# A graph attention layer on one core: where the constants of the attention scores are made

## What is computed

```python
self_feat = vcq @ W_self.T + b_self               # vcq: features and condition, 1024
for d in range(2):
    A = adj_f if d == 0 else swapaxes(adj_f, 1, 2)
    A = A[:, :, :20, :]                           # 20 keys
    qh = (self_feat @ Wq[d].T + bq[d]).reshape(B, N, 16, 32)
    kh = (self_feat[:, :20] @ Wk[d].T + bk[d]).reshape(B, 20, 16, 32)
    aff = einsum('bnhd,bmhd->bnhm', qh, kh) / sqrt(32)
    aff = where(A.sum(-1) > 0, aff, -9e15) + (A @ w_bias + b_bias)
    output += softmax(aff) applied to self_feat[:, :20] and Wout[d], + bout[d]
return x + relu(output)
```

## Time and profile before

| | us |
|---|---|
| median of 3 runs | 1914.61 (1913.51 to 1915.31) |
| profiled execution | 1915.0, span 1913.2, TensorE's mean granted clock 0.986 |
| TensorE matmuls busy | 1864.9 (97%) |
| TensorE weight loads busy | 1668.7 (87%) |
| VectorE, ScalarE, GpSimd busy | 1103.0, 1005.8, 725.4 |
| DMA | 255.59 MB, mean 134 GB/s |
| chain that ended last | TensorE 92% |
| of it L1562, L1575, L1542, L1540 | 30%, 20%, 10%, 3% |

### The profile page before, as it was taken

How to read it: one execution, slowest core, us unless ns; L and a number is a source line. 1 busy time by engine, 2 the same in 40 slices (tenths; PEclk the granted TensorE clock), 3 DMA queues, 4 the chain that set the end, 5 groups by cost and what they waited for, 6 DMA issues and landing times.

```text
span 1913.2 us, 46955 instructions
## 1 busy us (share of the span) xinstructions
PE 1864.9 (97%) x15864; PEld 1668.7 (87%) x15864; DVE 1103.0 (58%) x1937; ACT 1005.8 (53%) x1717; POOL 725.4 (38%) x617
## 2 busy tenths in 40 slices
PE   8999998879999999999999999999999999999997
PEld 5899998868888888888888888888888888888886
DVE  2433232456666666666666666666666666666632
ACT  2333232235556666666565566555666666656543
POOL 0322222004444444444444444444444444444444
PEclk9999999979999999999999999999999999999999
DMA  6123334444546565555555555565565555555431
GB/s 198 46 83 89 91 96 104 110 115 141 155 137 159 144 156 144 149 144 144 144 144 145 144 157 151 152 154 147 143 159 146 152 142 147 144 145 145 120 93 63
DMA packets 263747, 255.59 MB, mean 134 GB/s; under 512 B 78192, under 2 KB 194160, under 8 KB 263536
## 3 DMA queue, kind: packets, MB, share of 16 engines
q1 hardware_dynamic: 259360, 252.84, 49.4%
q10 hardware_dynamic: 4176, 0.02, 0.1%
HBM read 197.94 MB, written 54.79 MB: 132 GB/s over the span
## 4 chain that ended last, share of the span: by engine, by line
PE 92%; SPq 1%; DVE 1%; issue 1%; ACT 1%; DMA 0%; POOL 0%; POOLq 0%; DVEq 0%; ACTq 0%
PE bank L1562 30%; PE bank L1575 20%; PE low_banks L1542 10%; PE low_banks L828 9%; PE bank L1596 8%; PE bank L828 4%; PE bank L1588 4%; PE low_banks L1540 3%; PE bank L1563 2%; PE bank L1604 1%; SPq L640 1%; ACT kx L1437 0%; DVE zc L1267 0%; DMA k_dram<-kv_kst 0%; SPq L1078 0%
## 5 line engine op out<-in xcount | busy, mean ns | idle before, releaser
L1562 PE MATMUL bank<-kx,xt_main 128*128 128x160 f32 x4096 | 635.9, 304 | 0.3 <-ACT kx L1437 0.3
L1562 PEld LDWEIGHTS bank<-kx,xt_main 128*128 128x128 f32 x4096 | 583.8, 192 | 7.4 <-issue 0.9
L1437 ACT ACTIVATE kx<-low_banks 128x1280 f32<-128x1280 f32 (+3 forms) x268 | 318.2, 1187 | 259.1 <-PE low_banks L1542 259.1
L1388 POOL TENSOR_TENSOR res<-res,xk 128x512 f32<-128x512 f32 x128 | 163.9, 1280 | 669.6 <-ACT res L1427 669.6
L1280 DVE TENSOR_TENSOR sc<-bank,masks 128x320 f32<-128x320 f32 x256 | 125.8, 491 | 398.8 <-PE bank L1563 396.9
L1542 PE MATMUL low_banks<-key_tile,a_rows 32*128 32x160 f32 (+3 forms) x4288 | 220.7, 320 | 14.6 <-ACT kx L1437 8.9
L1575 PE MATMUL bank<-ws_h,xh_main 128*128 128x512 f32 x512 | 222.2, 434 | 2.5 <-DVE res L1306 2.5
L1370 POOL TENSOR_TENSOR sc<-sc,mx 128x640 f32<-128x640 f32 x128 | 160.2, 1272 | 152.1 <-DVE mx L1292 152.1
L1432 ACT ACTIVATE zc<-low_banks 128x1280 fp32r<-128x1280 f32 (+2 forms) x67 | 79.7, 1190 | 244.3 <-PE low_banks L1540 244.3
L1575 PE MATMUL bank<-ws_l,xh_main 128*128 128x512 f32 x512 | 203.1, 397 | 0.0
L1575 PE MATMUL bank<-ws_h,xl_main 128*128 128x512 f32 x512 | 203.0, 397 | 0.0
(11 more groups left out here) (144 smaller groups left out, 3085.4 us busy)
## 6 DMA issues: line engine op xcount, KB each, us to landing
rows_main<-in_x SPq DMA_DIRECT2D x256, 128.0 KB, 6.3
xs<-in_x SPq DMA_DIRECT2D x64, 512.0 KB, 4.8
xk<-in_x SPq DMA_DIRECT2D x64, 512.0 KB, 3.7
res<-c_dram SPq DMA_DIRECT2D x64, 512.0 KB, 7.2
out<-res SPq DMA_DIRECT2D x128, 256.0 KB, 3.1
adj<-in_mask_BxSxSx_ik SPq DMA_DIRECT2D x32, 440.0 KB, 8.2
adj<-in_mask_BxSxSx_ik SPq DMA_DIRECT2D x128, 110.0 KB
vbd<-v_dram SPq DMA_DIRECT2D x768, 10.0 KB
```

Source lines behind the costliest of these rows:

```text
L1388: pool.tensor_tensor(res[:, p.par, b, :], res[:, p.par, b, :], xk[:, p.par, b, :], ALU.add).then_inc(res_ready, 1)
L1437: nc.scalar.activation(taken(kx[:, t.par, j], lo, hi), generated(0, P, lo, hi), ACT.Copy).then_inc(gen_taken, 1)
L1562: mm = nc.tensor.matmul(dst, xt[:, j, p.ring + b, :], kx[:, t.par, j, :, :, w, :].rearrange("p r c m -> p c r m"), start=(j == 0), stop=False)
```

## The change

The constants are made in the keys stage. There the key is still in `kst`: ScalarE multiplies it by the query bias, GpSimd by the batch's condition query, both into `prod`. VectorE turns the blocks of 32 and sums 32 values each into `zs`; ScalarE and GpSimd split the sums into a high and a low part in `zz`; VectorE turns them so that they lie in rows, and SP stores them in `z_dram` with 8 DMAs at the end of each half, ahead of the next half's row loads. In the window loop step 0, its copy and its subtraction are gone, and so is `condition_columns`. Two DMAs a slot load four rows for each batch of the pair (`load_constants`) into `zc`, which now has four places and is cleared once. The order of the tiles in SBUF is another, and of the early loads those of the edges and of the first row sums come later: in half 7, behind the second key store (`late_loads`). The mask of the second edge direction is made by VectorE in slot -1.

```diff
@@ keys_and_values
+            sp.wait_ge(z_turned, n + 1)
+            for r in range(NQ):
+                for e in range(2):
+                    o = Q * r + ZQ * e
+                    sp.dma_start(v["z_dram"][r, e::2, bass.ds(n * HALF, HALF)].rearrange("c (q i) -> q c i", i=Q),
+                                 zt[o:o + MQ]).then_inc(z_stored, 16)
@@ SP, half 7
+                if last and p == 2:
+                    sp.wait_ge(pe_feat, C * HALVES)
+                    sp.wait_ge(f_low, C * HALVES)
+                    v["late_loads"](sp)
@@ VectorE
+        def constant_sums(n, p):
+            dve.wait_ge(by_bias, NK * n + p + 1)
+            dve.wait_ge(by_condition, NK * n + p + 1)
+            if due(NK * n + p):
+                dve.wait_ge(z_summed, NK * n + p)
+            nc.vector.transpose(pt[:], prod[:, p % 2].rearrange("p k (q i) -> p (k q) i", i=Q)).then_inc(p_turned, 1)
+            dve.wait_ge(p_turned, NK * n + p + 1)
...
+            nc.vector.tensor_reduce(zs[:, p].rearrange("p k q -> p (k q)"), pt[:], AX.X, ALU.add).then_inc(z_summed, 1)
+            constant_sums(n, 0)
+            for j in range(C):
+                constant_sums(n, 1 + j)
+                if not last:
                     features_out(n + 1, 1 - par, j)
+            constant_sums(n, 5)
             if not tail:
                 turn_x(blk + 1, n + 2, par)
...
                 nc.vector.transpose(vt[:, m % 4], vst[:, m % 2]).then_inc(v_turned, 1)
+                if m < 2:
+                    constant_sums(n, 6 + m)
+            turn_constants(n)
@@ GpSimd
+        def by_conditions(n, p):
+            pool.wait_ge(kv_out, 2 * NK * n + p + 1)
+            if due(NK * n + p - 1):
+                pool.wait_ge(p_turned, NK * n + p - 1)
+            pool.tensor_tensor(prod[:, p % 2, 1, :] ... kst ... cq ..., ALU.mult).then_inc(by_condition, 1)
+            by_conditions(n, 0)
+            by_conditions(n, 1)
             if not last:
                 conditions(n + 1)
-                features_low(n + 1, 1 - par)
+            for j in range(C):
+                by_conditions(n, 2 + j)
+                if not last:
+                    feature_low(n + 1, 1 - par, j)
+            by_conditions(n, 6)
+            by_conditions(n, 7)
...
+            constants_low(n)
@@ ScalarE
             if due(16 * (4 * n + p // 2)):
                 act.wait_ge(k_stored[p % 2], 16 * (4 * n + p // 2))
+            if due(NK * n + p - 1):
+                act.wait_ge(by_condition, NK * n + p - 1)
+                act.wait_ge(by_bias, NK * n + p - 1)
...
+        def by_biases(n, p):
+            act.wait_ge(kv_out, 2 * NK * n + p + 1)
+            if due(NK * n + p - 1):
+                act.wait_ge(p_turned, NK * n + p - 1)
+            nc.scalar.activation(prod[:, p % 2, 0, :], kst[:, p % 2, :], ACT.Copy,
+                                 scale=bq_all[:, p:p + 1]).then_inc(by_bias, 1)
             for j in range(C):
                 key_out(n, par, C + j)
+                by_biases(n, C + j)
                 if not last:
                     feature_high(n + 1, 1 - par, j)
@@ window_loop
+    def load_constants(sp, p):
+        for b in range(2):
+            o = (2 * p.n + b) * NG
+            sp.dma_start(zc[ZK * b:ZK * b + ZK, p.c % AGES, :].bitcast(F32).rearrange("k (h m) -> k h m", m=NG),
+                         v["z_dram"][:, :, bass.ds(o, NG)].rearrange("r (p k) m -> k (r p) m", k=ZK)
+                         ).then_inc(zc_loaded[p.par], 16)
@@ SP, slot
+                if t.back(4).real():
+                    sp.wait_ge(pe_s, scored(t.back(1), 3))
+                load_constants(sp, t)
@@ TensorE
-                pe.wait_ge(zl_ready, 2 * (t.n + 1) if t.real() else 2 * PAIRS)
-            elif step == 1:
-                pe.wait_ge(z_low, t.n + 1)
-                    if step == 0:
-                        mm = nc.tensor.matmul(low_banks[:, r, dst], zl[s, o, :], rhs, start=True, stop=True)
             if a == 0:
+                pe.wait_ge(zc_loaded[p.par], 32 * (p.half + 1))
-            if has_window(nxt):
-                generate(nxt, 0)
```

More of the change, by code:

```diff
@@ L141, in build @@
         kv_out = sem("kv_out")
+        z_stored = sem("z_stored")
         with ExitStack() as third:
-            windowed, early_loads, early_turn = window_loop(nc, scope(third)[0], sem, bank, low_banks, locals())
+            windowed, early_loads, late_loads, early_turn = window_loop(nc, scope(third)[0], sem, bank, low_banks, locals())
         with ExitStack() as keyed:
@@ L680, in turn_x, with turn_constants @@
                                 j).then_inc(x_turned, 1)
+        def constant_sums(n, p):
[5 more added lines that the diff above has]
+            dve.wait_ge(p_turned, NK * n + p + 1)
+            if p == 0 and due(n):
+                dve.wait_ge(z_high, n)
+                dve.wait_ge(z_low, n)
+            nc.vector.tensor_reduce(zs[:, p].rearrange("p k q -> p (k q)"), pt[:], AX.X, ALU.add).then_inc(z_summed, 1)
+        def turn_constants(n):
+            dve.wait_ge(z_low, n + 1)
+            if due(n):
+                dve.wait_ge(z_stored, 16 * 2 * NQ * n)
+            nc.vector.transpose(zt[:], zz[:].bitcast(F32).rearrange("p c h k q -> p (c h k q)")
+                                .rearrange("p (b i) -> p b i", i=Q)).then_inc(z_turned, 1)
         def one_half(blk, n, par, first, last, tail):
@@ L684, in one_half @@
                 pick_condition(n + 1)
-            if not last:
                 nonzero(n + 1, 1 - par)
-                for j in range(C):
+            constant_sums(n, 0)
+            for j in range(C):
+                constant_sums(n, 1 + j)
+                if not last:
                     features_out(n + 1, 1 - par, j)
+            constant_sums(n, 5)
             if not tail:
@@ L1135, in nonzero_rows @@
         spread = nzm[:].rearrange("p w z -> p (w z)")
-        for o in (0, Q):
-            a = p.ring * (P + 1) + o
-            nc.vector.tensor_scalar(spread[:, a:a + P + 2:P + 1], sums[:], 0.0, None,
+        for o in (1, 3):
+            a = p.ring * P + o
+            nc.vector.tensor_scalar(spread[:, a:a + P + ZK + 1:P + ZK], sums[:], 0.0, None,
                                     ALU.not_equal).then_inc(nz_ready, 1)
@@ L1260, in vector_program @@
     def vector_program(dve):
-        def constants_low(t):
-            dve.wait_ge(z_high, t.n + 1)
-            lo, hi = window(t)
-            o = taken(zc[Q:ZR, t.par], lo, hi)
-            nc.vector.tensor_tensor(o, generated(Q, ZR, lo, hi), o.bitcast(F32), ALU.subtract).then_inc(z_low, 1)
+        nc.vector.memset(zc[:].bitcast(F32), 0.0).then_inc(set_once, 1)
+        nc.vector.memset(nzm[:], 0.0).then_inc(set_once, 1)
+        dve.wait_ge(set_once, 2)
+        for b in range(2):
+            for o in (0, 2):
+                nc.vector.memset(nzm[:, b::2, ZK * b + o:ZK * b + o + 1], 1.0).then_inc(set_once, 1)
         def add_masks(t, a):
@@ L1309, in slot @@
             soft, late = t.back(3), t.back(4)
-            nxt, after = t.back(-1), t.back(-2)
+            nxt = t.back(-1)
             if soft.real():
@@ L1333, in slot @@
                 nonzero_rows(dve, nxt)
-            if after.real():
-                condition_columns(dve, after)
             g = edge_group(t if t.c % 2 == 0 else t.back(1))
-            if due(g) and has_edges(g):
+            if has_edges(g) and (due(g) or t.c % 2):
                 count_and_weigh(dve, g, t.c % 2)
```

158 lines of the change are left out of this document (86 added, 72 removed).

## The result

The kernel after takes 1925.47 us (median of 4 runs, 1923.86 to 1928.36), the kernel before 1914.06 (4 runs beside it): a ratio of 1.0063, 95% interval 1.0045 to 1.0080. It is slower, by 11.4 us; the interval is 8.6 to 15.3 us. The profiled execution of after took 1923.86 us with a span of 1922.0, against 1915.0 and 1913.2 of before.

The account below looks back on a forecast made before the run. The prediction took TensorE to bound both long stages. From the profiled 1915.0 us, -42.5 for the removed step and +61 for the keys stage, with zero for hand-over and loads, gave 1933.5 us, range 1897 to 1962.

Parts of the forecast that it names:

- a closed round on SP and the key steps: Keys stage: SP's stores and loads plus steps from key to key close a circle of 48.5 us a half instead of 36.4.
- case E: Whole kernel: the forecast itself, 1933.5 us, with its own range 1919 to 1950; chance 0.55.
- The slot, -34: Window loop: the removed 0.76 us step gives 0.57 a slot, as 0.1 to 0.2 returns as a wait; 34 us in 60.
- The ramp, -7: Ramp into the window loop: five steps and their waits fall out, new waits come; -7 us, bounds -14 and +5.
- The drain, -1.5: Drain: the two steps left, 0.6 us each, go with their hand-overs; -1.5 us.
- The key steps: Keys stage: transpose, product, cast, subtraction, product and hand-overs take 3.8 us from key to key; 20.5 to the first value store.
- The halves: Keys stage: +12 us in each of halves 3 to 5, less in the others; sum 64.5, taken as 61.
- The slack of 0.8 us: Keys stage: the third key's copy ends 14.7 us into the half, its bank is needed at 15.5; 0.8 us of slack.
- case B: Keys stage: dearer transposes or stores, and TensorE at the lower clock after every stall; +25, 1958 us; chance 0.17.
- A: Keys stage: products and turns fit in the gaps, only SP's stores push; +22, so 1894.5 us, faster; chance 0.19.
- C: Window loop: the constants' loads are late, TensorE waits up to 0.6 us a slot; 1967 us; chance 0.03.
- D: Whole kernel: loss and gain cancel, 45 and 45; 1915 us, within 0.2%; chance 0.06.

Follow-up runs that it names:

- slot_order: The kernel after, in the window loop alone ScalarE's copy of the late weights moved ahead of the first exponential: 1903.12 us.
- neither: The kernel after without the keys stage's products, casts, transposes, sums and stores of constants; one transfer fills the constants, which are wrong: 1851.64 us.
- no_products: The kernel after without the key products and their transposes and sums; split, turn and stores of constants stay: 1880.60 us.
- no_constant_stores: The kernel after without the eight stores of constants a half; products, sums and turn stay, one transfer fills the constants: 1895.42 us.
- gpsimd_order: The kernel after with GpSimd's products of keys 3 and 4 ahead of its first subtraction of features in the keys stage: 1895.61 us.
- before_slot_order: The kernel before, only with ScalarE's copy of the late weights ahead of the first exponential in the slot: 1911.23 us.
- key_stores_on_scalar: The kernel after with the key stores issued by ScalarE, each behind its product, instead of by SP: 1854.57 us.
- both_orders: The kernel after with key stores issued by ScalarE and the late weights' copy ahead of the first exponential in the slot: 1831.89 us.
- four_buffers_gpsimd_order: The kernel after with four key buffers instead of two and GpSimd's products of keys 3 and 4 ahead of its first subtraction: 1868.21 us.

## Why the prediction was right, and where not

It gave 1933.5 us with a range of 1897 to 1962 and slower as the likely sign; measured 1925.47. The mechanism (a closed round on SP and the key steps) is the one that the runs show, and it was the likeliest case E (1919 to 1950). That the total came within 8 us is in part luck, since misses cancel in the keys stage and in the slot. Term by term:

**The slot, -34, measured -36.7: right for two reasons that cancel.** The chain over maxima, shift, exponential and copy came back as foreseen, but at 0.30 us, not 0.1 to 0.2. And the removed step was worth more than its 0.76 in the earlier trace rows: with the wait taken out (`slot_order`) the slot is 23.181 - 22.272 = 0.909 us shorter. The other 0.15 is around the step. TensorE in before at that place (start, length):

```profile
1012.74 0.34 PE L1563 MATMUL bank<-zc,flags 128*128 128x160 f32 x1
1013.01 0.82 PE L1540 MATMUL low_banks<-key_tile,zl 32*128 32x160 f32 x16
1013.77 0.55 PE L1588 MATMUL bank<-identity,wt 128*128 128x128 f32 x3
1014.15 0.84 PE L1562 MATMUL bank<-kx,xt_main 128*128 128x160 f32 x5
```

And in `slot_order`, without the step:

```profile
1014.77 0.34 PE L1650 MATMUL bank<-zc,flags 128*128 128x160 f32 x1
1014.95 0.49 PE L1675 MATMUL bank<-identity,wt 128*128 128x128 f32 x3
1015.28 0.98 PE L1649 MATMUL bank<-kx,xt_main 128*128 128x160 f32 x6
```

By the starts, the closing matmul of the scores took 0.27 us to the next instruction instead of 0.18, and the three transposes 0.38 instead of 0.33; the means over the slots between 600 and 1700 us are the same. So 0.91 - 0.30 = 0.61, where I had 0.76 - 0.19 = 0.57; my upper bound of 0.76 for the step was too low.

**The ramp, -7, measured -12.7.** Its waits on the chain copy, subtraction, next step went. The new ones in after are TensorE's 5.25 us for a copy on ScalarE that stands behind the load of the row sums, 2.49 for the flags and 2.27 for the second mask; none is for the constants. I had set too much against the gain for late loads. In `neither` the ramp is 60.9 us, so the additions of the keys stage cost 6 us here too. They cost it together: with the turn and stores alone (`no_products`) it is 62.7, with the products alone (`no_constant_stores`) 63.6.

**The drain, -1.5, measured -2.0: not shown.** After's order of the slot ran in nine profiles, and their drains took 69.2 to 71.7 us, with the same waits of TensorE in after and `neither` (8.5 us). What differs is the granted clock: in a stretch that begins 20 to 25 us ahead of the end it was 0.50 for 3.4 us in after, 6.8 in before and 10.2 in `neither`. So the 2.0 us can't be put on the two removed steps.

**The key steps.** 3.8 us from key to key, measured 3.60; 20.5 us from the first key store to the first value store, measured 20.46 and 20.59; the transpose of 128x640 0.86, measured 0.833; the sum 0.8, measured 0.820; the products 0.46 and 0.88, measured 0.563 and 0.729. Value stores 16.2, measured 16.8 and 15.4.

**The stores of constants: mis-sized.** 5.2 us for eight, measured 3.60 (0.45 each), and 3.17 outside the loop. I had taken the price near that of the row load, for its two strided dimensions; they cost what the value stores do. Against it stood a term that I did not have: 3.16 us between the last of these stores and the row loads where the loop starts over (below), once in the stage; without the stores it is 0.73.

**The halves.** From first key store to first key store, after less before: 6.8, 6.5, 9.6, 14.1, 11.2, 5.8 and 5.9 us, against 1.5, 6.5, 12, 12, 12, 8.5 and 8.5 in my order. The sum is 59.9, mine 61 without the last value's 3.5 (TensorE's wait ahead of the first window matmul grew by 3.0, from 0.57 to 3.61). The distribution was off at both ends, and the sum is nearer than its terms: in the three rounds from half 2 to half 5 the stores were too dear by 1.6 us each, and against it stood the 2.4 us of the longer gap and 2.1 us more ahead of the first value store of half 2 (22.56 instead of 20.5), neither of them foreseen. In the first, both parts count already (46.2 us in `no_constant_stores`, 45.5 in `no_products`, 42.3 in `neither`). TensorE's stops are 9.7, 11.6 and 7.6 us in halves 3 to 5, near the 8 to 12 that I named as the sign. ScalarE's wait for the key store is 17.6 to 21.5 us there (over 15 named).

**The slack of 0.8 us.** I read that a new store may be up to 0.8 us late per half at no cost. `no_products` shows that such slack is spent once, not in each half. SP of before behind the earlier trace rows:

```profile
215.41 15.88 SPq L640 DMA_DIRECT2D v_dram<-kv_vt  x32
232.02 6.00 SPq L70 DMA_DIRECT2D rows<-in_x  x8
238.29 11.13 SPq L634 DMA_DIRECT2D k_dram<-kv_kst  x8
```

From the key store at 201.86 to that at 238.29 SP's own round was 13.55 + 16.61 + 6.27 = 36.43 us, just TensorE's half of 36.4 (the next one was 35.5). So the round had almost no room. In `no_products` TensorE does not stop in halves 1 and 2, where the first key store comes 11.7 and 12.7 us into TensorE's half (8.4 and 9.5 in before); in half 3 it comes 16.0 us into it (12.3 in before). From there on TensorE stops in every half, for 3.1, 6.6, 3.0, 2.3 and 3.0 us: 3.6 on average, the whole length of the eight stores, where I had 2.8. The longest is in the half with the longer gap where the loop starts over.

**Low clock.** I had it in case B only, as an addition. It is in the result (15.1 us of busy time), but by the account of the round it adds nothing to the sum: SP's round sets the half, and stop and slow matmuls share the room in it. That is argued; no run separates the two.

**Rivals.** A (the circle does not close, only the stores push, +22): `no_products` shows that mechanism alone at 26.1 us, so its price was near, though with cheaper stores in more halves than I had; it fell because a key step costs 3.6 us. The limit of 2.3 us that I gave for it does not hold: with steps of 2.23 us (`gpsimd_order`) the keys stage is still 325.7 us, against 312.1 without products. C: no wait for the constants in the steady slots at all; the two loads cost SP 0.78 us a slot, under waits of 175.3 us for the value matmuls where the earlier trace rows had 238.4. On how many of the DMA engines they ran, no row shows. B (dearer parts) and D fell with the measured prices.

What stays open: the 2.9 us in the preparation, where the change edits nothing. In the eleven profiles with the code of after the first projection begins between 75.3 and 78.9 us, in the three with that of before between 78.6 and 79.5. So most of it may be spread, but not surely all; no run tests it.

## What to carry to other kernels

Where a queue's issues are ordered by hand, add up the queue's round as you do for an engine: in this kernel SP's was 36.43 us beside TensorE's 36.4, and TensorE's busy share told nothing of it. New work belongs at a place where the in-order engine waits anyway (the stores of constants behind the key stores, two products ahead of a subtraction that waits, the copy ahead of an exponential that waits), or on another queue. And a step taken off the bottleneck gives its time back only as far as the chain beside it allows; look which instruction stands needlessly behind that chain.

## What the runs showed of the hardware

- A step on the 32-row strips between matmuls on all 128 rows cost TensorE time beside the step itself: the matmul ahead of it took 0.275 us to the next start where it takes 0.184 ahead of a transpose, and the three transposes behind it 0.383 instead of 0.327 (means over 47 to 49 slots of before and `slot_order`), 0.15 us a slot. The Trainium skill, TensorEngine Tiling (Array Packing), Key Properties, says that changing the tiling mode drains TensorE; the rows agree in kind and give the size.
- SP's gap where its loop starts over was 0.72 to 0.74 us in the six kernels with 96 DMA issues in the loop's body (before, `before_slot_order`, `neither`, `no_constant_stores`, `key_stores_on_scalar`, `both_orders`), and 2.90 to 3.22 us in the seven with 112. What the row loads wait for, VectorE's turns, was done at 241.6 in after, 24 us before them. Its cause was not tested.
- Behind six of the seven stops in after's keys stage, those of 4.6 to 11.6 us, TensorE took 0.27 us from matmul to matmul instead of 0.147, at a granted clock of 0.50, for 3.2 to 5.9 us; behind the stop of 2.5 us it was 0.147 at 1.00. In `no_products` the granted clock was 0.50 behind stops of 2.3 to 3.1 us too, and in `four_buffers_gpsimd_order` it stayed at 1.00 behind stops of 1.2 to 2.8. In sum TensorE's busy time in after's keys stage was 15.1 us above that of `neither`.
- A DMA issue on ScalarE's queue took 0.34 to 0.37 us, and ScalarE's next cast began 0.12 us later for it: 0.59 us (median) behind the start of its product, against 0.47 in after.
